# Two post-norm transformer layers on one Trainium2 core: the first expert tile in quarters around the gate, and a reordered last batch

## The reference, cut to what matters

```
x1 = LN(x + linear_attention(x))        # per batch: a 256x256 matrix made from all 1024 tokens
p  = softmax(x1 @ gate_w + gate_b)      # 8 experts; those under 0.1 dropped, the rest renormalised
x2 = LN(x1 + sum_e p[:, e] * (x1 @ expert_w[e] + expert_b[e]))
x3 = LN(x2 + head_attention(x2))        # 16 heads of 16; scores between the HEADS of one token
s  = x3 @ w_router                      # the 768 best of a batch's 1024 tokens:
y  = LN(x3 + where(top768(s), gelu(x3 @ w_block), x3))
```

## Time and profile before

| | before |
|---|---|
| three runs | 1431.96, 1433.84, 1435.29 us, median 1433.84 |
| profiled execution | 1434.45 us; span 1432.6, so 1.85 us lie around the span |
| mean granted TensorE clock | 0.855 |
| busy | PE 84%, DVE 64%, ACT 51%, POOL 40% |
| chain that ended last | PE 53%, DVE 18%, POOL 7%, no wait shown 7%, DMA 6%, ACT 6% |
| 160 us from 676 | PE 146.31, DVE 112.79, ACT 89.99, POOL 70.49 us busy |

### The profile page before, as it was taken

One profiled execution on the slowest core, in us unless ns is written; L12 is line 12 of the kernel. 1 busy time (PEld: TensorE's weight loads), 2 busy tenths in 40 slices (PEclk: granted clock), 3 DMA queues, 4 the chain that ended last, 5 costly groups with the idle time before them and its releaser, 6 DMA issues.

```text
span 1432.6 us, 31148 instructions
## 1 busy us (share of the span) xinstructions
PE 1202.3 (84%) x12264; PEld 760.1 (53%) x12264; DVE 915.9 (64%) x2113; ACT 733.3 (51%) x1156; POOL 570.2 (40%) x887
## 2 busy tenths in 40 slices
PE   6689899997999899988999899988999898784443
PEld 3444456654665556654665556654665545442442
DVE  3534666587677866587677866587677776464534
ACT  3222465347554765357554675357454675356423
POOL 3125326425424525435424525435524515331312
PEclk8579998899879988899879987899879987787566
DMA  5000090205411190206410290207420290209220
GB/s 177 15 1 15 30 161 4 75 15 148 60 32 45 70 152 3 75 16 148 60 46 31 86 136 2 75 16 154 54 60 2 79 128 2 59 16 168 24 60 30
DMA packets 93145, 90.64 MB, mean 63 GB/s; under 512 B 7110, under 2 KB 81864, under 8 KB 92744
## 3 DMA queue, kind: packets, MB, share of 16 engines
q1 hardware_dynamic: 81736, 76.06, 26.8%
q0 software_dynamic: 2560, 8.39, 1.7%
q10 hardware_dynamic: 8704, 4.20, 1.1%
HBM read 46.68 MB, written 41.94 MB: 62 GB/s over the span
## 4 chain that ended last, share of the span: by engine, by line
PE 53%; DVE 18%; POOL 7%; issue 7%; DMA 6%; ACT 6%; SPq 2%; ACTq 1%; POOLq 0%; DVEq 0%
PE bank L1512 50%; DVE keys L1296 3%; POOL rs L521 2%; DVE x L1201 2%; DVE gelu L1298 2%; DVE stats L1060 2%; ACT x L793 1%; PE bank L1522 1%; DMA scratch_qkv<-part 1%; DMA scratch_qkv<-stage 1%; DMA bt<-scratch_o 1%; DVE ct L1030 1%; DMA scratch_o<-stage 1%; POOL stage L572 1%; DMA ct<-scratch_qkv 1%
## 5 line engine op out<-in xcount | busy, mean ns | idle before, releaser
L1512 PE MATMUL bank<-we,at 128*128 128x512 f16 x1536 | 365.5, 399 | 0.0
L1512 PEld LDWEIGHTS bank<-we,at 128*128 128x128 f16 x1536 | 154.0, 102 | 191.9 <-issue 36.4
L536 POOL TENSOR_TENSOR part<-part 128x512 f32<-128x512 f32 x64 | 83.0, 1297 | 353.8 <-ACTq L819 353.8
L671 ACT ACTIVATE part<-bank,wexp 128x256 f32<-128x256 f32 x256 | 105.2, 471 | 185.7 <-PE bank L1512 124.2
L1201 DVE SCALAR_TENSOR_TENSOR x<-bank,wexp,x 128x256 f32<-128x256 f32 x256 | 122.9, 480 | 81.0 <-PE bank L1512 75.0
L1512 PE MATMUL bank<-bt,wqkv 128*128 128x512 f16 x576 | 139.7, 385 | 15.6 <-DVE stage L1030 12.9
L793 ACT ACTIVATE x<-x,nm,rs 128x256 f32<-128x256 f32 x192 | 104.6, 593 | 92.5 <-POOL nm L524 91.2
L517 POOL TENSOR_SCALAR nm<-mv 128x2 f32<-128x2 f32 x128 | 32.3, 252 | 254.0 <-DVE mv L1065 248.5
L1030 DVE TENSOR_TENSOR stage<-bank,stage 128x512 f16<-128x512 f32 x112 | 75.6, 686 | 85.3 <-ACT stage L671 85.0
L1512 PE MATMUL bank<-keys,blockdiag 128*128 128x16 f16 x3072 | 96.6, 193 | 24.3 <-DMA keys<-scratch_qkv 18.5
L1512 PEld LDWEIGHTS bank<-keys,blockdiag 128*128 128x128 f16 x3072 | 95.6, 104 | 29.5 <-DMA keys<-scratch_qkv 19.0
(11 more groups left out here) (176 smaller groups left out, 2268.8 us busy)
## 6 DMA issues: line engine op xcount, KB each, us to landing
scratch_qkv<-stage SPq DMA_DIRECT2D x40, 512.0 KB, 3.8
ct<-scratch_qkv SPq DMA_DIRECT2D x128, 128.0 KB, 5.7
x_in<-in_x_dram SPq DMA_DIRECT2D x32, 256.0 KB, 2.7
keys<-scratch_qkv SPq DMA_DIRECT2D x64, 128.0 KB, 5.1
bt<-scratch_o SPq DMA_DIRECT2D x16, 512.0 KB, 3.7
out_dram<-x POOLq DMA_DIRECT2D x32, 256.0 KB, 2.7
scratch_qkv<-part SPq DMA_DIRECT2D x8, 512.0 KB, 8.2
scratch_o<-stage SPq DMA_DIRECT2D x32, 128.0 KB, 3.5
```

The costliest lines, as they stand in the source:

```text
L536: pool.tensor_tensor(part[:, 0:2, :], part[:, 0:2, :], part[:, 2:4, :], ALU.add)\
L671: return act.activation(dst, src, ACT.Copy, scale=scale)
L1512: ins = pe.matmul(dst, lhs, rhs, start=(n == 0), stop=(n == len(terms) - 1))
```

## The change

1. PE computes the expert tile 0 of batch a at the end of the turn in which its gate is computed, in quarters: q 0 ahead of WT, q 1 and 2 ahead of BIAS0, q 3 ahead of BIAS2. It leaves the next turn's start. DVE and ACT evict it ahead of what they did there: DVE ahead of the spread of Q, ACT ahead of GRAM0's copy.
2. SP stores V's second part (F11) ahead of K's loads, in batches 0 to 6.
3. The linear attention's last transpose (TX3) is evicted earlier: on ACT ahead of `b_res(c, 1)`, on DVE ahead of `b_ff(c, 1)`. ACT also copies TX1 of batch b ahead of two `b_res`.
4. Last batch (7): SP no longer loads Q; ACT issues Q's 8 loads behind its eviction of F7. K's loads stand ahead of the stores of V. POOL turns Q's half 1 and ACT V's half 0, so that both halves are turned at once; the counts are split by half for it.
5. Last batch's feed-forward: PE's matmuls stand ahead of the ranks' matmuls; ACT computes all four GELUs into the free `x_in` before any `b_res`; each engine then has the four pairs in a row.

```diff
+            def b_loads(b):                       # SP, last batch only
+                b_f(b, 1)
...
+                b_f(b, 7)
+                b_loadk(b)
+                b_f(b, 9)
+                b_f(b, 11)
+                b_loadv(b)
...
                     b_f(b, 7)                     # SP, other batches
                     b_f(b, 9)
+                    b_f(b, 11)
                     b_loadk(b)
-                    b_f(b, 11)
                     b_loadv(b)
...
+                elif c is not None:               # POOL, last turn
+                    b_turnq(c, 1)
...
+            def b_gelu(b, p):                     # ACT
+                act.wait_ge(ff_full, 4 * b + p + 1)
+                act.activation(x_in[:, 2 * p:2 * p + 2, :].rearrange("p t n -> p (t n)"), m_bank[p][:, :],
+                               ACT.Gelu_apprx_tanh, scale=1.0 / WS).then_inc(ff_read, 1)
...
                     b_turnq(c, 0)                 # ACT, start of a turn
-                    b_turnq(c, 1)
+                    if b is not None:
+                        b_turnq(c, 1)
+                if b is not None:
+                    a_moe(b, 0)
                 if a is not None:
                     a_gram(a, 0)
...
                     b_f(b, 7)                     # ACT
+                    if b == NB - 1:
+                        b_loadq(b)
                     b_f(b, 8)
...
+                if b is not None:                 # DVE, start of a turn
+                    a_moe(b, 0)
                 if c is not None:
                     b_spreadq(c, 0)
-                if b is not None:
-                    a_moe(b, 0)
...
                 if a is not None:                 # PE, end of a turn
+                    a_moe(a, 0, (0,))
                     a_wt(a)
+                    a_moe(a, 0, (1, 2))
                     a_bias(a, 0)
                     a_bias(a, 1)
+                    a_moe(a, 0, (3,))
                     a_bias(a, 2)
                     a_bias(a, 3)
```

More of the change, by code:

```diff
@@ L205, in build_two_layer_postln @@
         v_loaded = sem("v_loaded")
-        q_turned = sem("q_turned")
-        v_turned = sem("v_turned")
+        q_turned = [sem(f"q_turned{hf}") for hf in range(2)]
+        v_turned = [sem(f"v_turned{hf}") for hf in range(2)]
         q_spread = [sem(f"q_spread{hf}") for hf in range(2)]
@@ L443, in b_loadv @@
                     sp.sem_inc(waits_held, 1)
-                sp.wait_ge(q_turned, 2 * b + 2)
+                for hf in range(2):
+                    sp.wait_ge(q_turned[hf], b + 1)
+                    sp.sem_inc(waits_held, 1)
                 for r in range(T):
@@ L622, in turn @@
                     a_sum(b, 7)
+                if b is None and c is not None:
+                    for p in range(TP):
+                        ln(c, 4 + p, 1)
+                        if p > 0:
+                            b_store(c, p - 1)
+                    b_store(c, TP - 1)
+                    return
                 if c is not None:
@@ L748, in b_pt @@
                 act.wait_ge(b_full, b_filled(b, f"PT{q}"))
-                act.wait_ge(v_turned, 2 * b + 2)
+                for hf in range(2):
+                    act.wait_ge(v_turned[hf], b + 1)
                 copy(pt_part(q, HI), b_ps(f"PT{q}")).then_inc(pt_hi, 1)
@@ L876, in turn @@
                     a_moe(b, 2)
+                elif c is not None:
+                    b_turnv(c, 0)
                 if c is not None:
@@ L925, in turn @@
                     b_rout(c, 1)
+                if b is None and c is not None:
+                    for p in range(TP):
+                        b_gelu(c, p)
+                    for p in range(TP):
+                        b_res(c, p)
+                    for p in range(TP):
+                        b_ffn(c, p)
+                    return
                 if b is None and c is None:
@@ L944, in turn @@
                     b_tx(b, 0)
+                if a is not None:
+                    to_at_hi(a, "TX3", 3, 3)
                 if c is not None:
@@ L1319, in b_ff @@
             def b_ff(b, p):
+                gelus = [x_in[:, 2 * p + t, :] if b == NB - 1 else gelu[:, t, :] for t in range(2)]
                 rows = [x3[:, 2 * p + t, :] for t in range(2)]
@@ L1323, in b_ff @@
                 for t in range(2):
-                    ins = dve.scalar_tensor_tensor(out=rows[t], in0=gelu[:, t, :],
+                    ins = dve.scalar_tensor_tensor(out=rows[t], in0=gelus[t],
                                                    scalar=msel[:, 2 * p + t:2 * p + t + 1], in1=rows[t],
@@ L1336, in turn @@
                 if c is not None:
+                    b_spreadq(c, 0)
                     b_spreadq(c, 1)
@@ L1382, in turn @@
                 if c is not None:
-                    b_pr(c, 0)
-                    b_pr(c, 1)
-                    b_pr(c, 2)
-                    b_pr(c, 3)
+                    for p in range(TP):
+                        b_pr(c, p)
                 if a is not None:
@@ L1433, in turn @@
                     b_tx(b, 0)
+                if b is None and c is not None:
+                    for p in range(TP):
+                        b_ff(c, p)
+                    return
                 if c is not None:
@@ L1636, in a_bias, with a_moe @@
                 ins.then_inc(a_full, 1)
-            def a_moe(a, t):
-                for q in range(4):
+            def a_moe(a, t, qs=range(4)):
+                for q in qs:
                     if t == 0 and later(a):
```

62 lines of the change are left out of this document (37 added, 25 removed).

## The result

| | before | changed |
|---|---|---|
| median of 4 runs | 1432.9 us | 1390.24 us (1386.09 to 1396.99) |
| ratio | | 0.9707, interval 0.9664 to 0.9751 |
| span of the profiled execution | 1432.6 | 1387.0 |
| mean granted TensorE clock | 0.855 | 0.879 |

A forecast was written before the change was run, and what follows sets the result against it. PE was taken to bound the kernel, with waits at gates and a low clock behind them. Terms 4.0 + 2 x 5.2 + 26.4 + 5.9 + 0 + 5.5 + 4.0 = 56.2 off 1434.45 gave 1378 us, range 1363 to 1397.

The forecast's parts named there:

- Part 1, the quarters: Turn ends, F11 to S0: 20.1 us; 6.6 less in four middle turns, 5.2 at batches 1 and 2, 4.0 at batch 0.
- What this needs of others: Middle turns: DVE's spread, K's and V's loads and POOL's turn of V come in time; gain bounded by 4.5 and 7.
- what comes behind S0 doesn't move up by as much: Rival: attention's waits for V, softmax and POOL grow, four middle turns give back 2 us each; 1388 us, chance 0.12.
- The case of 1390: Rival: the change works only in part, batch 7's and the last batch's terms are nil; 1390 us, chance 0.05.
- K's case: Rival: V's store delays K's landing beyond S0's former start, over 24.5 us; about 1436 us at 27, chance 0.03.
- DVE's cover: Middle turns: DVE's spread of Q, 5.38 us, is done by about 851, 2.9 us ahead of S0.
- Batch 7's turn: PT0, bound by S0 at about 10.4 us distance, comes 5.9 us sooner, between 3 and 7.
- V lands without POOL waiting: Sign for batch 7's turn: POOL, which waited 5.87 us for V before, no longer waits.
- Part 3: TX3's earlier eviction: PE's 1.72 us wait goes but F0 waits for DVE's bt; 0, with 0.3 either way a turn.
- Part 4: Last batch, Q loaded by ACT and halves turned on two engines: 5.5 us less, from -2.5 up to 9.
- Part 5: Last feed-forward, GELUs and PE's matmuls ahead of mres: 4.0 us less, 2.5 to 5.5.

The follow-up runs named there:

- E3: Changed kernel with expert tile 0 in one piece behind the biases, so the waits for gsel and w16t are not filled; ratio 0.9922.
- E9: The changed kernel run and profiled a second time, with no edit; S0 to F11 135.5 us.
- E1: The kernel before with only the quarters on PE and tile 0's earlier eviction added; S0 to F11 137.1 us.
- E4: Changed kernel with V's store behind K's loads again in batches 0 to 6; ratio 0.9811.
- E2: Changed kernel without the quarters of tile 0 on PE; S0 to F11 134.2 us, gain 1%.
- E5: Changed kernel with POOL's sum of tile 1 ahead of its turn of V's half 0; S0 to F11 134.9 us, lowest ratio measured.
- E12: Changed kernel with TX3's evictions behind the second pair's feed-forward, as before; first product to F0 8.61 us, against 8.62.
- E8: Changed kernel with the last batch's Q loaded by SP again, halves still turned on two engines; ratio 0.9720.
- E10: Changed kernel with the last feed-forward's reordering undone; the end takes 36.6 us, against 33.1.
- E6: E5's edit on the changed kernel, with V's half 1 also turned right behind half 0 on POOL; no gain over E5.
- E7: Changed kernel with every second load of V left out in all batches, so only half of V is loaded; 138.8 us behind S0.

## Why the prediction was right, and by how much it was off

The time lies in the range of 1363 to 1397, but 12 us above the forecast, and two errors partly cancelled in it. The mechanism of part 1 was right; that the rest of a middle turn would stay as it was, was not.

**Part 1, the quarters.** Right in mechanism and size: 20.2 us from F11 to S0 (20.1), 37.4 us over six turns (36.8), 4.8 up to the second gate (4.0; in the other kernels with the quarters it is 2.3 to 7.5, so that the 4.8 is not known well). E3 shows that it is the filling of the waits.

**What this needs of others: the step that failed.** Of V's loads the prediction says "they can go near 845 and V be there before POOL turns it at about 856", and of POOL's turning of V that "this has slack too", so the way behind S0 had 0 in the sum. They did go early, 10.4 us after F11 (forecast 11). But the landing was taken with no sharing. K's and V's loads now follow each other without a gap, V lands 24.1 us after F11 where the forecast needed it by 22, and the step measured -13.7: a turn takes 156.2 us, where 153.5 was to show. The slack was looked for at POOL's products, some 10 us after S0. What it hung on was the buffer `ct`: ACT writes its first transposed probabilities there once both halves of V are turned, at S0 + 14.3 before and S0 + 16.0 now. By the fitted line these 1.7 us are 1.6 of the 2.3 that a turn grew; in E9 it grew by 1.9.

E1 and E4 move the landing and the turn follows it; E2 and E3 give V its time back and the turn is nearly as before; E5 moves the turning alone and wins 0.6 to 1.0 us of it. This is the rival "what comes behind S0 doesn't move up by as much", given a chance of 0.12. It had been put down to waits in general, where the rows that decide it could have been asked for: POOL turned V at 859.87, and V landed at 859.71 (its last load's landing event), 0.16 us ahead; over the six turns this slack was 0.2 to 1.9 us.

That the rival's 1388 is nearly the time that came is partly luck. It gave back 2 us in each of four middle turns and 2 of parts 4 and 5; measured, six turns gave back 2.3 each and part 4 brought 4.6 more than forecast. The case of 1390, with nothing from batch 7's turn and the last batch, has the time too but did not happen: these brought 4.5, 10.1 and 3.3. Nor did K's case: K landed 5.2 us ahead of S0.

**DVE's cover** of 2.9 us was smaller than said, since POOL's sums of tile 0 now lie beside the spread, and it took 7.36 instead of 5.38. It still ended 1.0 ahead of S0. S0 waited for neither `keys` nor `blockdiag` in the six turns.

**Batch 7's turn**: 4.5 for 5.9, within its bounds of 3 and 7. From F11, S0 came 2.4 us sooner (about 3 was said) and the first PT 12.3 us behind S0, where 10.4 was forecast and 13.2 measured before. "V lands without POOL waiting" failed: POOL waited 8.38 for V and turned it from S0 + 4.4, before from S0 + 5.6.

**Part 3**: 0, as said, for the reason given (E12).

**Part 4**: 10.1 for 5.5. The forecast had S0 1.5 us later than before and the way behind it 7.0 shorter; measured, S0 came 5.1 sooner and the way behind it was 5.0 shorter. The term mis-sized was Q's landing: taken 3.1 us longer from its issue than the 12.8 before, it was 2.9 shorter. In the other kernels with Q's loads on ACT it took 9.1 to 12.5 us, with them on SP 12.8 in all three (before, E1 and E8), so the gain varies, and what in the queue makes the difference was not taken apart. F7's store is the steadier part: it lands in 4.2 to 5.4 us when Q's loads are on ACT and in 8.7 to 8.9 behind them on SP, and K's loads wait for it. By E8 these two together are 3.1 of the 5.1 us up to S0 and 2.0 of the 5.0 behind it. The other 5.0 are there in E8 too, most of them (3.0) behind S0, where two engines turn the halves. E1, without any of part 4, has 1.0 of these as well.

The rule of the Trainium skill that was cited (page "DMA: Bandwidth & Descriptors", section "Issuing engines are not separate DMA queues") holds in its first half, that such transfers share the engines and interleave. The trace agrees: F7's store, issued by SP at 1264.11, landed in 4.9 us among Q's loads of ACT, and F3's, ahead of them, in 2.7. Its second half, that issuing from several engines saves issue time only, doesn't hold here: F7's store lands 6.4 us later in E8, counted from the first FF, of which 2.5 are issue time (SP was still issuing Q's loads) and 3.9 are its longer landing. The Trainium skill's same page says in its section "Queues, rings and completion order" that a DMA engine goes in turn between the queues that it has work for. By that rule a store on SP's queue needn't wait for loads on ACT's, and the trace agrees (5.0 us for 8.9).

**Part 5**: 3.3 for 4.0 (E10).

The sum was 56.2; measured stretch by stretch it is 45.6, or 56.2 + 0.8 + 0.6 - 13.7 - 1.4 + 4.6 - 0.8 - 0.7. The errors of part 4 and of V's landing have opposite signs, and that they partly cancel is luck.

**Left open.** PE's clock is at 0.50 for 17 to 31 us of the stretch behind S0, by turns, and the scatter goes with it in part; why one turn has more of it than another was not tried. Nor was why E6, with ACT's copy earliest of all the kernels with part 1, gains nothing over E5.

## What to carry to other kernels

Where work is pulled forward, list what lands by DMA for it and compare the landings, not the issues: an engine that didn't wait for a transfer may have had less than a us of slack. Filling a wait of under 2 us on TensorE can bring more than twice its length (6.5 us for the 2.5 of two waits here), where the granted clock falls behind it, and only the fill does it, not the move (E3). When a store and loads share one issuing queue, look at what waits for the store.

## What the runs showed that was not expected

A copy of 128x2048 f16 on POOL that starts within DVE's four masked copies of that size stretches them from 2.73 to 7.38 us (E7), and in one turn of E3 to 6.24; the same four take 2.73 while POOL waits. The trace's view of the tile `blockdiag` gives the four in E7 apart, minimum, median and maximum in ns:

```profile
L1287 DVE TENSOR_SCALAR blockdiag<-shared,const x4: 742/1252/4371, 838.9 to 844.5; 128x2048 f16<-128x2048 f16 x4
```

One of them takes 4.37 us, which is its own 0.74 and nearly all of POOL's 3.86; the next takes 1.76, beside the sum that POOL goes on with. The Trainium skill has this on its page "SBUF — State Buffer", section "Who interferes with whom": `tensor_scalar` on VectorE in its faster modes and GpSimd share a port pair that one of them holds for its whole instruction while the other stands still. The trace agrees with such a standstill, by the 4.37 us; the port itself no run shows. In the changed kernel POOL's three sums take 1.78, 1.06 and 1.06 us beside eight such operations instead of 1.25, 0.73 and 0.73 later in the turn, and the eight 7.36 instead of 5.38. An earlier landing can thus cost more than a late one (138.8 us behind S0 in E7, 136.0 in the changed kernel).
